# A second transfer queue at both ends of the front, and a reordered begin, last layer and tail of the expert stage

## The reference, cut to what matters

```python
xn = layernorm(x) * ln_w + ln_b
xi, z = split(xn @ W_in)                       # 256 channels each
u = silu(conv1d(xi, 4 taps) + conv_b)
dt, B, C = split(u @ W_xproj)                  # 8, 64, 64
delta = softplus(dt @ W_dt + b_dt)
h_t = h_{t-1} * exp(delta_t * A) + (delta_t * u_t) * B_t      # state 256 x 64, 1024 steps
y_t = sum_n(h_t * C_t) + u_t * D
x1 = layernorm(x + (x + (y * silu(z)) @ W_out))
v = x1
for l in range(4):
    p = softmax(v @ router_w[l] + router_b[l]); comb = top2(p), normalised
    xhat = layernorm(v)
    y_e = gelu((xhat * g[l,e] + b[l,e]) @ w1[l,e] + b1[l,e]) @ w2[l,e] + b2[l,e]
    v = sum_e comb_e * (v + y_e)
out = layernorm(x1 + v)
```

## Time and profile before

| | |
|---|---|
| three runs, us | 2242.24, 2242.97, 2248.36; median 2242.97 |
| the profiled execution | 2246.93, of which the span of the trace is 2245.1 |
| busy: PE, DVE, ACT, POOL | 95%, 82%, 71%, 41% |
| granted TensorE clock, mean | 0.98 |
| DVE scan, L1519 | 512 times 2309 ns, 1157.0 us together |
| PE first() and second(), L1294 and L1306 | 385.4 and 475.9 us |
| HBM read, written | 67.98 MB, 45.88 MB |

### The profile page before, as it was taken

The page is one execution under the profiler, slowest core; times in us unless marked ns, Lnnn a source line. Parts: engine busy times, 40 slices in busy tenths (PEclk is TensorE's granted clock), DMA queues, the critical chain, the costliest instruction groups (busy, mean ns, idle before and its releaser), DMA issues. The chain is left out here.

```text
span 2245.1 us, 50361 instructions
## 1 busy us (share of the span) xinstructions
PE 2130.0 (95%) x16960; PEld 1258.0 (56%) x16960; DVE 1838.6 (82%) x2779; ACT 1596.8 (71%) x2070; POOL 920.4 (41%) x452
## 2 busy tenths in 40 slices
PE   7968999999999999999999997999999999999997
PEld 3432333333333333333333335999999999999986
DVE  6869999999999999999999996566555566556665
ACT  5868888888888888888888883545455455445543
POOL 3123334343443444343434344444444444444442
PEclk9977999999999999999999998999999999999999
DMA  5995222222222121212121234000100010000000
GB/s 171 279 281 136 43 46 45 42 46 41 45 42 46 41 46 40 46 40 46 40 46 40 47 96 135 1 0 0 38 1 0 0 39 1 0 1 1 10 11 18
DMA packets 354957, 114.93 MB, mean 51 GB/s; under 512 B 283000, under 2 KB 345600, under 8 KB 354624
## 3 DMA queue, kind: packets, MB, share of 16 engines
q1 hardware_dynamic: 350416, 110.92, 20.2%
q10 hardware_dynamic: 4464, 3.02, 0.4%
HBM read 67.98 MB, written 45.88 MB: 51 GB/s over the span
## 5 line engine op out<-in xcount | busy, mean ns | idle before, releaser
L1519 DVE TENSOR_TENSOR_SCAN arena<-behind 128x1040 f32<-128x1040 f32 x512 | 1157.0, 2309 | 21.1 <-ACT behind L961 18.2
L1062 ACT ACTIVATE arena<-PS,arena 128x512 f32<-128x512 f32 x512 | 342.9, 688 | 399.5 <-PE PS L1294 398.9
L951 ACT ACTIVATE behind<-PS 128x1024 f32<-128x1024 f32 x512 | 526.7, 1029 | 133.9 <-DVE arena L1519 101.3
L1197 PE MATMUL PS<-arena 128*32 128x128 f32 x8192 | 565.9, 406 | 0.0
L961 ACT ACTIVATE behind<-PS 128x1024 f32<-128x1024 f32 x512 | 539.4, 1053 | 20.0 <-PE PS L1180 16.3
L1306 PEld LDWEIGHTS PS<-arena 128*128 128x128 f32 x4096 | 475.8, 193 | 8.1
L1306 PE MATMUL PS<-arena 128*128 128x128 f32 x4096 | 475.9, 276 | 0.0
L771 POOL COPY behind<-carry 128x64 f32<-128x64 f32 x128 | 206.1, 1611 | 518.1 <-DVE arena L1519 384.2
L1294 PE MATMUL PS<-parts_xh,parts_w 128*128 128x512 f32 x1536 | 385.4, 402 | 14.7 <-ACT arena L1062 14.7
L1197 PEld LDWEIGHTS PS<-arena 128*32 128x32 f32 x8192 | 234.6, 119 | 288.1 <-issue 210.9
L1180 PE MATMUL PS<-arena 96*128 96x512 bf16 x1024 | 314.3, 389 | 66.5 <-ACT behind L961 34.6
(11 more groups left out here) (131 smaller groups left out, 1381.5 us busy)
## 6 DMA issues: line engine op xcount, KB each, us to landing
dl_d<-arena SPq DMA_DIRECT2D x48, 256.0 KB, 3.5
du_d<-arena SPq DMA_DIRECT2D x48, 256.0 KB, 3.6
arena<-dl_d SPq DMA_DIRECT2D x512, 24.0 KB
arena<-b_d SPq DMA_DIRECT2D x64, 192.0 KB
arena<-du_d SPq DMA_DIRECT2D x512, 24.0 KB
b_d<-arena SPq DMA_DIRECT2D x48, 128.0 KB, 2.8
u_d<-behind SPq DMA_DIRECT2D x8, 512.0 KB, 3.9
sz_d<-arena SPq DMA_DIRECT2D x8, 512.0 KB, 4.8
```

What stands on the lines that cost most here:

```text
L951: nc.scalar.activation(seg(dA[:, half])[:, :, 1:], PS[:, 0:2, :].rearrange("p j (i t) -> p (j i) t", t=TC), ACT.Exp).then_inc(exp_done, 1)
L1062: nc.scalar.activation(hT[:, e % 2, c], PS[:, HIDDEN[(GT * e + c) % 3], :], ACT.Gelu, bias=bias1[:, lp, e * GT + c:e * GT + c + 1]).then_i ...
L1197: last = nc.tensor.matmul(PS[32 * j:32 * j + 32, 4 + kk, 0:DB], cd[:, pair, j, 32 * i:32 * i + 32], seg(hb[kk])[:, :, 1 + 16 * j + i], sta ...
L1519: nc.vector.tensor_tensor_scan(hb[kk][:, q * QD * SEG:(q + 1) * QD * SEG], dA[:, q % 2], dB[:, G_, lo:lo + QD * SEG], 0.0, ALU.mult, ALU.a ...
```

## The change

At the front's start the eleven weights and the taps are parted: ACT issues w_in, taps, vecs, chan and w_xproj on its own queue, SP the identity, a_log and w_dt, and after x of items 2 and 3 the four that only later stages use, which have a semaphore of their own (later_weights). DVE runs moments and norm of item 0, then both of item 1. At the front's end the stores of u and silu(z) of the last two items and the first block's load_products are issued by ACT; the memset of rhs_u[0] runs an item earlier; second_part(6) comes after the last Ln; steps(7) ahead of the third part of item 6; first_part_delta(7), first_part_du(7) and PE's turn_du(7) come between the first four products. In the expert stage ACT's stage_norm(0) comes ahead of evacuate(1) and the load of b2. In group 0 stage_norm(1) and stage_norm(2) come ahead of experts 2 and 3, and transposes and split of group 1 later. In the last layer finish is two parts, finish_moments behind add_expert(0) and finish_norm behind add_expert(1). The last group is finished in two halves of two tiles, with the upper half of its last product in another PSUM bank, and its stores wait for each half.

The diff, without context; a header gives the line before the change and the place. New semaphores (later_weights, y_first) are left out, and leading blanks are cut.

```diff
@@ L406, constants
-WEIGHTS = 16 * 11
+WEIGHTS, LATER_WEIGHTS = 16 * 7, 16 * 4
@@ L486, shared helpers
+def y_bank(n, e, s):
+    apart_from_first = isinstance(n, int) and n == NL * NG - 1 and e == E - 1 and s >= GT // 2
+    return 5 if apart_from_first else Y_BANK[e]
@@ L492, shared helpers
+def load_products(eng, c, pair, kk):
+    it, o = pair * 2 + c // CPT, c % CPT * NOCT
+    eng.dma_start(Bst[kk][0:ROWS], b_d[it].rearrange("(o e) b p n -> (e b p) o n", e=OCT)
+                  [:, bass.ds(o, NOCT), :]).then_inc(du_in[kk], 16)
+    src = du_d[it].rearrange("b p (o e) (k d) -> e k (b p) o d", e=OCT, d=DB)
+    for e in range(OCT):
+        eng.dma_start(rhs_u[kk][RW * e:RW * e + RW, :, e, :], src[e, kk, :, bass.ds(o, NOCT), :]
+                      ).then_inc(du_in[kk], 16)
+def store_rows(eng, k):
+    it, bb = k // 2, k % 2
+    eng.wait_ge(a_sz, k + 1)
+    eng.wait_ge(a_u, k + 1)
+    for dram, v in ((u_d, u_s), (sz_d, sz_s)):
+        eng.dma_start(dram[it, bb].rearrange("(h p) t -> p h t", p=P), v[bb]).then_inc(a_stored[bb], 16)
@@ L513, sync: start
-    sp.dma_start(taps_s.rearrange("p t d -> p (t d)"), taps).then_inc(taps_in, 16)
@@ L515, sync: start
-    for dst, src in ((al, a_log.rearrange("(h p) n -> p h n", p=P)), (ident_s[:], ident), (vecs_s[:], vecs),
-                     (chan_s[:], chan),
-                     (win_s, w_in), (wx_s, w_xproj.rearrange("(h p) n -> p h n", p=P)),
-                     (wdt_s[N:N + R, :], w_dt), (wout_s[:], w_out.rearrange("(h p) n -> p h n", p=P)),
-                     (rb_s[:], router_b), (g_s[:], ln_g), (lb_s[:], ln_b)):
+    for dst, src in ((ident_s[:], ident), (al, a_log.rearrange("(h p) n -> p h n", p=P)),
+                     (wdt_s[N:N + R, :], w_dt)):
@@ L522, sync: start
+    for dst, src in ((wout_s[:], w_out.rearrange("(h p) n -> p h n", p=P)),
+                     (rb_s[:], router_b), (g_s[:], ln_g), (lb_s[:], ln_b)):
+        sp.dma_start(dst, src).then_inc(later_weights, 16)
@@ L530, sync: start
-    def load_products(c, pair, kk):
...
@@ L573, sync: loop over items
-        sp.wait_ge(a_sz, k + 1)
-        sp.wait_ge(a_u, k + 1)
-        for dram, s in ((u_d, u_s), (sz_d, sz_s)):
-            sp.dma_start(dram[it, bb].rearrange("(h p) t -> p h t", p=P), s[bb]).then_inc(a_stored[bb], 16)
+        if k < ITEMS - 2:
+            store_rows(sp, k)
@@ L583, sync: loop over items
-        if k == LAST:
-            sp.wait_ge(clear_u[0], 1)
-            load_products(0, 0, 0)
@@ L594, sync: loop over items
-            load_products(0, 0, 1)
+            load_products(sp, 0, 0, 1)
@@ L620, sync: blocks
-            load_products(nc_, np_, nk)
+            load_products(sp, nc_, np_, nk)
@@ L663, sync: stores of the result
-    with sp.Fori(0, NG // 2) as g2:
+    def store_out(g, gp, s):
+        sp.dma_start(tokens(out, g * 2 + s // 2, s % 2), xo[:, gp, s, :]).then_inc(f_out[gp], 16)
+    with sp.Fori(0, NG // 2 - 1) as g2:
@@ L669, sync: stores of the result
-                sp.dma_start(tokens(out, g * 2 + s // 2, s % 2), xo[:, gp, s, :]
-                             ).then_inc(f_out[gp], 16)
+                store_out(g, gp, s)
+    sp.wait_ge(f_fin, NG - 1 + FIN0)
+    for s in range(GT):
+        store_out(NG - 2, 0, s)
+    for s in range(GT):
+        sp.wait_ge(f_fin, NG + s // 2 + FIN0)
+        store_out(NG - 1, 1, s)
@@ L743, gpsimd: loop over items
-        if k == LAST:
-            pool.wait_ge(a_zp, ITEMS)
+        if k == LAST - 1:
+            pool.wait_ge(a_tp, ITEMS)
+            pool.wait_ge(a_xn, ITEMS)
@@ L747, gpsimd: loop over items
+        if k == LAST:
+            pool.wait_ge(a_zp, ITEMS)
@@ L858, gpsimd: expert stage
+        if isinstance(layer[0], int) and layer[0] == NL - 1 and not (isinstance(g, int) and g == 0):
+            rsqrt(rs_o, o_var, o_rs, g)
@@ L862, gpsimd: expert stage
-        if isinstance(layer[0], int) and layer[0] == NL - 1 and not (isinstance(g, int) and g == 0):
-            rsqrt(rs_o, o_var, o_rs, g)
@@ L867, gpsimd: expert stage
-    rsqrt(rs_o, o_var, o_rs, NG)
+    rsqrt(rs_o[:, 0:GT // 2], o_var, o_rs, NG)
+    rsqrt(rs_o[:, GT // 2:], o_var, o_rs, NG + 1)
@@ L871, scalar: start
+    act.dma_start(win_s, w_in).then_inc(weights, 16)
+    act.dma_start(taps_s.rearrange("p t d -> p (t d)"), taps).then_inc(taps_in, 16)
+    for dst, src in ((vecs_s[:], vecs), (chan_s[:], chan), (wx_s, w_xproj.rearrange("(h p) n -> p h n", p=P))):
+        act.dma_start(dst, src).then_inc(weights, 16)
@@ L919, scalar: loop over items
+        if k >= ITEMS - 2:
+            store_rows(act, k)
@@ L925, scalar: loop over items
+        if k == LAST:
+            act.wait_ge(clear_u[0], 1)
+            for i in range(2):
+                act.wait_ge(a_rows[i], ROW_STORES)
+            load_products(act, 0, 0, 0)
@@ L936, scalar: loop over items
-        if k > 0:
+        if 0 < k < LAST:
@@ L1007, scalar: ahead of and behind the blocks
+    second_part(LAST - 1)
@@ L1013, scalar: ahead of and behind the blocks
-    first_part_delta(LAST)
-    first_part_du(LAST)
+        if r == 1:
+            first_part_delta(LAST)
+        if r == 2:
+            first_part_du(LAST)
+    act.wait_ge(later_weights, LATER_WEIGHTS)
@@ L1017, scalar: ahead of and behind the blocks
-    evacuate(NC - 1, BP - 1, 1)
-    act.dma_start(b2_s, b2.rearrange("p (l e h) -> p l e h", l=NL, e=E)).then_inc(b2_in, 16)
@@ L1052, scalar: expert stage
-            if isinstance(n, int) and n == 0 and e == 1:
+            begins = isinstance(n, int) and n == 0
+            if begins and e == 2:
@@ L1054, scalar: expert stage
-            if more and e == 2:
+            if more and e == (3 if begins else 2):
@@ L1066, scalar: expert stage
-    run_layers(act, lambda first_layer: stage_norm(0, 0, 0), step)
+    def begin(first_layer):
+        stage_norm(0, 0, 0)
+        evacuate(NC - 1, BP - 1, 1)
+        act.dma_start(b2_s, b2.rearrange("p (l e h) -> p l e h", l=NL, e=E)).then_inc(b2_in, 16)
+    run_layers(act, begin, step)
@@ L1259, tensor: ahead of the blocks
-    turn_du(LAST)
+        if r == 1:
+            turn_du(LAST)
@@ L1261, tensor: ahead of the blocks
+    pe.wait_ge(later_weights, LATER_WEIGHTS)
@@ L1306, tensor: expert stage
-                last = nc.tensor.matmul(PS[:, Y_BANK[e], s * P:(s + 1) * P], hT[:, e % 2, c, s * P:(s + 1) * P],
+                last = nc.tensor.matmul(PS[:, y_bank(n, e, s), s * P:(s + 1) * P], hT[:, e % 2, c, s * P:(s + 1) * P],
@@ L1307, tensor: expert stage
+            if isinstance(n, int) and n == NL * NG - 1 and e == E - 1 and s == GT // 2 - 1:
+                last.then_inc(y_first, 1)
@@ L1334, tensor: expert stage
-        if more:
+        if more and not begins:
@@ L1338, tensor: expert stage
+        if begins:
+            stage_xh(1, 1)
@@ L1405, vector: start
-    for k in range(2):
@@ L1448, vector: loop over items
+        if k == LAST:
+            steps(k)
@@ L1453, vector: loop over items
-        steps(k)
+        if k < LAST:
+            steps(k)
@@ L1535, vector: ahead of the blocks
+    dve.wait_ge(later_weights, LATER_WEIGHTS)
@@ L1691, vector: expert stage
-    def finish(g, gp):
+    def finish_moments(g):
@@ L1698, vector: expert stage
+        moments(f_fl, g * O_LINKS + 1, lambda s: xsum_o[:, s], st_o, mv_o, rs_o, GT, o_var)
+    def finish_norm(g, gp):
@@ L1701, vector: expert stage
-        moments(f_fl, g * O_LINKS + 1, lambda s: xsum_o[:, s], st_o, mv_o, rs_o, GT, o_var)
@@ L1704, vector: expert stage
+    def finish_half(half):
+        g, n = NG - 1, NG * NL - 1
+        lo, hi = half * GT // 2, (half + 1) * GT // 2
+        if half == 0:
+            dve.wait_ge(x_in, 32)
+            dve.wait_ge(f_fin, g + FIN0)
+            dve.wait_ge(f_out[1], 64 * (g // 2) + 64)
+            dve.wait_ge(f_x0, n + 2)
+            dve.wait_ge(f_sum, FS0 + E * n + E - 1)
+            dve.wait_ge(y_first, 1)
+        else:
+            dve.wait_ge(f_y, FY0 + E * n + E)
+        for s in range(lo, hi):
+            last = nc.vector.scalar_tensor_tensor(at(X, g, s), PS[:, y_bank(n, E - 1, s), s * P:(s + 1) * P],
+                                                  comb[:, 1, s * E + E - 1:s * E + E], at(X, g, s),
+                                                  ALU.mult, ALU.add)
+        last.then_inc(f_last, 1)
+        dve.wait_ge(f_last, 3 + half)
+        links = g * O_LINKS + half * O_LINKS
+        tiles = lambda v: v[:, g * GT + lo:g * GT + hi, :]
+        nc.vector.tensor_tensor(xsum_o[:, lo:hi], tiles(X), tiles(X1), ALU.add).then_inc(f_fl, 1)
+        dve.wait_ge(f_fl, links + 1)
+        moments(f_fl, links + 1, lambda s: xsum_o[:, lo + s], st_o[:, lo:hi], mv_o[:, lo:hi], rs_o[:, lo:hi], GT // 2,
+                o_var)
+    def finish_half_norm(half):
+        lo = half * GT // 2
+        dve.wait_ge(o_rs, NG + half)
+        scaled_apart(lambda s: xsum_o[:, lo + s], mv_o[:, lo:], rs_o[:, lo:], lambda s: xo[:, 1, lo + s], GT // 2
+                     ).then_inc(f_fin, 1)
```

(19 more changed lines are left out.)

13 lines of the change are left out of this document (4 added, 9 removed).

## The result

The changed kernel takes 2226.85 us (median of six; 2225.70 to 2231.06), the kernel before 2244.30 (median of six; 2240.86 to 2248.36). The ratio is 0.9924, 95% interval 0.9912 to 0.9935. The profiled execution of the changed kernel took 2226.26, with a span of 2224.5.

The account below looks back on a forecast made before the run. Bounds: full DMA engines and two tied paths in the front, DVE in the scans, PE in the expert stage. Terms +0.9 (front), -7.0, -5.4, -4.7 sum to -16.2, from 2242.97 to 2226.8 us; range 2218 to 2235.

Parts of the forecast that it names:

- Part 1: Begin of the front: 2.5 us later (1.8 to 3.3), from the norms' order 1.8 and x landing later 0.7.
- Part 2: End of the front: store stream gains only idle engine time, 1.6 us; first scan 4 earlier, then waits at the ninth.
- Part 3: Begin of the expert stage: PE's stalls of 3.22 and 3.93 go, 5.78 remains; gain 7.0 us (5.1 to 8).
- Part 4: Last layer: finish() leaves DVE's serial chain, so groups take 25.69 us throughout; gain 5.4 us (4.5 to 5.5).
- Part 5: Tail after PE's last product: finishing in halves leaves two store issues of four; gain 4.7 us (4 to 5).
- (a): Front: the queue is the limit, SP's stream up to 7.9 us earlier, front gains 4, total 2222; chance 0.25.
- (b): Start of the expert stage keeps half its stalls, gaining 3 us instead of 7, total 2231; chance 0.13.
- (c): Block loop: PE enters at 1.2 GHz, 10 us more per such block, 2247 with two; chance 0.04.
- (d): End of the front: a late new wait (clear_u[0] on ACT) keeps the first scan; within 1 us; chance 0.58 with forecast.

Follow-up runs that it names:

- b_begin: Changed kernel with the old order of the norms and all weights and taps on SP's queue again; 2228.62 us, 0.9924 of the kernel before.
- f_tail: Changed kernel with the last group's finish in one piece and one set of output stores again; 2229.03 us, 0.9929 of the kernel before.
- g_norm0: Changed kernel keeping the early stage_norm(0), but norms and xh of groups 1 and 2 at their old places; 2234.07 us, 0.9948 of the kernel before.
- h_issues: Changed kernel with each dl_d and du_d store split in two of half the size; 2242.96 us, 0.9988 of the kernel before.
- c2_loads_sp: Changed kernel with only the nine loads of the first products back on SP; 2229.81 us, 0.9930 of the kernel before.
- c_end: Changed kernel with the whole end of the front undone; 2227.16 us, 0.9918 of the kernel before.
- d_hand: Changed kernel with the whole begin of the expert stage undone; 2236.12 us, 0.9956 of the kernel before.
- i_best: Changed kernel, norms' order restored, first block's loads on SP an item earlier, second block's on ACT, split_xh(1) before the router; 2219.81 us, 0.9894 of before.

## Why the prediction was right, and where it was not

The way and the size were right, and so were the mechanisms of parts 3 and 4. That the forecast, 2226.8, met the measured 2226.85 to the tenth is luck: the time it started from was 1.3 low (2242.97 against the later median of 2244.30) and the gain 1.3 small (16.2 against 17.45). Against its own profiled execution the sum was -16.2, and the two profiled executions differ by 20.67. Inside the sum, too, terms that were off cancelled.

- Part 1: the total was right (item 1's b_d 2.33 later; 2.5 predicted), and b_begin gives 2.0 down to the scans. Its parts were not. The order cost DVE 1.49 rather than 1.8, and x landed 0.18 later rather than 0.7; together that is 1.67 at the end of the taps' product (14.25 against 12.58). The rest came from PE's first x16 group, 9.05 instead of 8.40, which the sum does not have. It took from 8.46 (f_tail) to 9.54 (g_norm0) in traces with the very same front and from 8.57 to 9.70 in those with the order restored, so it is scatter and not shown to come from the change.
- Part 2: the argument, that the engines are full and only their idle time can be won, held (h_issues, c2_loads_sp). The Trainium skill says the same of second queues ("DMA: Bandwidth & Descriptors", Issuing engines are not separate DMA queues): they save only the issuing time, so where the engines are full the u/sz stores had to bring nothing, which c2_loads_sp agrees with (133.05 against c_end's 132.83). Two terms were mis-sized. The stream gained 3.0 and not 1.6: the share was counted only between 154 and 162, where it rose by 0.18; in 110 to 154 it also went from 1.01 to 1.03, and from 291 to 303 GB/s, over 44 us, an estimated 0.9 more. What gave the remaining 0.5 is open. And the nine loads cost ACT 9.05, not 5. The price was that of SP's own loads (4.50 for eight at 156.07 in the kernel before), but ACT issues them beside SP's stream and behind its own stores, at 1.09 each. So the first scan came at 170.66 instead of 167.5, and the 5 us of idle time at the ninth never was. The front gained 0.7 to the ninth scan (1.0 to the x96 group) instead of losing 0.9.
- Part 3: -7.43 for -7.0. Of the 7.43, d_hand gives 6.28 to the reorder; the other 1.15 lies between two executions of the same instructions. What was late next is as said, DVE's split behind the router (it ends at 1403.54, group 1 starts at 1403.68); the stall that remained is 6.45, where 5.78 was expected to stay.
- Part 4: the last layer's own gain is 5.45 (210.47 to 205.02), 5.4 predicted. The other 1.6 of the table is one turn of layers that took 32.48 before and 30.87 after, though nothing of it changed.
- Part 5: -5.18 for -4.7, but the 4.7 was not all the halves'. Part of it comes from finish(6) being gone, which is part 4's edit: 1.9 without the halves, and 3.3 more with them.
- The rivals: (a) a stream up to 7.9 shorter did not come (3.0). In i_best it is 5.0 shorter (128.28). (b) half the stalls back: no, d_hand and g_norm0 give 6.3 and 3.3. (c) PE did not stay at 1.2 GHz: the level is 0.50 until 194 as before, and its mean over the block loop 1.00 in both. (d) no wait on clear_u[0] shows, but its effect, a first scan that hardly moves, came by another way: ACT held by its own issues.

## What to carry to other kernels

Before moving transfers to an idle engine's queue, look at the DMA share where they will be issued: beside a stream that already fills the engines the issue itself is held, and what stands behind it in that engine's program pays. Here a load cost the second queue 0.77 to 1.09 and the first, with engines about as full, 0.62 to 0.72. Where two paths end together, neither is worth shortening alone, and an undoing of one edit doesn't measure it; here two edits that gave nothing singly gave 2.0 together by the traces. Single edits that move work from one of the two paths to the other do not prove a tie. At the end of a program, cost two edits of the same chain together, as the first to be undone takes the other's gain with it.
